# One expert's overflow rows take their second product in another place, and the tiles of finished rows get eight homes

## The reference

```
ys  = cond / sqrt(512);  d = rsqrt((ys*ys) @ (Wc*Wc) + 1e-8)
xf  = ((x * ys) @ Wc) * d                     # x: 2 x 2048 x 512, 4096 tokens
top = argmax(softmax(xf @ gate_w.T))          # one of two experts per token
for e in 0, 1:
    masked = where(top == e, xf, 0)           # other tokens' rows are zero
    routed += relu(masked @ w1[e] + b1[e]) @ w2[e] + b2[e]
shared = relu(xf @ sw1 + sb1) @ sw2 + sb2     # 512 -> 2048 -> 512
out = x + routed + shared
```

## Time and profile before

| | |
|---|---|
| median of 3 runs | 1408.11 us (1404.99 to 1409.16) |
| profiled execution, its own time | 1408.37 us |
| its span (first to last instruction) | 1406.6 us |
| PE busy | 1367.4 us, 97% of the span |
| DVE, ACT, POOL busy | 1004.5, 679.7, 364.2 us |
| mean granted PE clock | 0.990 |
| DMA in the span | 334.54 MB, 238 GB/s |
| chain that ended last | PE 86%, DMA 6%, DVE 4%, issue 2% |

### The profile page before, as it was taken

The page is one execution under the profiler, slowest core; times in us unless marked ns, Lnnn a source line. Parts: engine busy times, 40 slices in busy tenths (PEclk is TensorE's granted clock), DMA queues, the critical chain, the costliest instruction groups (busy, mean ns, idle before and its releaser), DMA issues.

```text
span 1406.6 us, 17366 instructions
## 1 busy us (share of the span) xinstructions
PE 1367.4 (97%) x5990; PEld 1126.0 (80%) x5990; DVE 1004.5 (71%) x1424; ACT 679.7 (48%) x988; POOL 364.2 (26%) x328
## 2 busy tenths in 40 slices
PE   9999999999989999899999999999999999897997
PEld 7888888888868788787888888888888887785886
DVE  7979967667788967966557878777897758453331
ACT  4456644545455544665666444444564445231220
POOL 0000005544636544250000000000000032354884
PEclk9999999999999999999999999999999999998999
DMA  6967475776877578653668887978787899997762
GB/s 206 285 244 223 181 250 189 252 231 251 268 257 260 209 255 272 229 181 129 213 224 281 262 281 251 290 254 272 258 250 244 273 291 320 290 298 178 215 163 33
DMA packets 243449, 334.54 MB, mean 238 GB/s; under 512 B 71760, under 2 KB 106576, under 8 KB 243088
## 3 DMA queue, kind: packets, MB, share of 16 engines
q1 hardware_dynamic: 216592, 299.58, 64.7%
q0 software_dynamic: 21248, 30.30, 9.8%
q10 hardware_dynamic: 5520, 3.54, 0.8%
HBM read 201.25 MB, written 149.29 MB: 249 GB/s over the span
## 4 chain that ended last, share of the span: by engine, by line
PE 86%; DMA 6%; DVE 4%; issue 2%; POOL 1%; ACT 1%; POOLq 0%; DVEq 0%; ACTq 0%; SPq 0%
PE bank L2015 39%; PE bank L2093 30%; PE bank L2122 8%; PE bank L1943 6%; DMA rows<-xf_scratch,quad_tab 1%; DMA y_rows<-x_rows,tab 1%; DMA hin<-hidden_scratch 1%; DMA out<-y_rows,tab 1%; DMA hin<-expert_hidden 1%; DVE vb L1512 1%; PE bank L2034 1%; DVE xw L1448 0%; DMA y_rows<-sorted_rows_out 0%; PE bank L2135 0%; DVE hl L1479 0%
## 5 line engine op out<-in xcount | busy, mean ns | idle before, releaser
L2015 PE MATMUL bank<-xw,w_hi 128*128 128x512 f32 x1792 | 555.9, 392 | 14.3 <-DVE vb L1512 12.2
L2093 PE MATMUL bank<-hl,w_hi 128*128 128x512 f32 x1344 | 414.4, 389 | 2.4 <-DVE hl L1479 2.2
L2015 PEld LDWEIGHTS bank<-xw,w_hi 128*128 128x128 f32 x1792 | 337.9, 189 | 86.8 <-DVE vb L1512 13.8
L1479 DVE TENSOR_TENSOR hl<-hin,hl 128x512 fp32r<-128x512 f32 x400 | 265.1, 686 | 197.5 <-ACT hl L1037 189.9
L1037 ACT CAST hl<-hin 128x512 fp32r<-128x512 f32 x400 | 244.6, 621 | 323.0 <-PE bank L2093 185.1
L2015 PE MATMUL bank<-xw,w_lo 128*128 128x512 f32 x896 | 350.4, 391 | 0.0
L2093 PEld LDWEIGHTS bank<-hl,w_hi 128*128 128x128 f32 x1344 | 251.8, 188 | 56.5 <-issue 3.5
L2093 PE MATMUL bank<-hl,w_lo 128*128 128x512 f32 x672 | 261.4, 389 | 0.0
L2015 PEld LDWEIGHTS bank<-xw,w_lo 128*128 128x128 f32 x896 | 169.3, 189 | 35.7
L1061 ACT ACTIVATE vb<-bank,b 128x512 f32<-128x512 f32 x192 | 130.2, 688 | 115.9 <-PE bank L2015 92.7
L882 POOL DMA_INDIRECT rows<-xf_scratch,quad_tab x128 | 129.6, 1012 | 150.4 <-PE bank L2015 105.2
(11 more groups left out here) (199 smaller groups left out, 1337.1 us busy)
## 6 DMA issues: line engine op xcount, KB each, us to landing
hin<-hidden_scratch SPq DMA_DIRECT2D x168, 512.0 KB
hidden_scratch<-vb SPq DMA_DIRECT2D x120, 512.0 KB
hidden_scratch<-vt SPq DMA_DIRECT2D x48, 512.0 KB
hin<-expert_hidden SPq DMA_DIRECT2D x32, 512.0 KB
w_new<-w_shared SPq DMA_DIRECT2D x52, 256.0 KB, 5.4
expert_hidden<-vb SPq DMA_DIRECT2D x24, 512.0 KB
ring<-x_cols SPq DMA_DIRECT2D x32, 256.0 KB
xf_scratch<-xo SPq DMA_DIRECT2D x32, 256.0 KB, 4.8
```

Of the source, the lines that this page charges most:

```text
L1479: nc.vector.tensor_tensor(hl[:, n % HL, 1, :], hin[:, n // 2 % LOADS, n % 2, :], hl[:, n % HL, 0, :].bitcast(F32), ALU.subtract).then_inc( ...
L2015: last = nc.tensor.matmul(up_bank(u, UP_BANK[c])[p][:], w[:, DOWN_W[c], pair, part], xw[:, c, x, k, :], start=(c in FRESH and n == 1), sto ...
L2093: last = nc.tensor.matmul(bank[p][:], w[:, DOWN_W[c], i, part], hl[:, n % HL, h, :], start=(i == 0 and q == 0), stop=(i == PAIRS - 1 and q ...
```

## The change

1. **Expert 0's overflow rows** go down from the weights of the seven products while those lie there: at the start of the last down block, (5, 0). `loose_set` on PE does 8 + 16 + 8 + 16 matmuls per unit and DVE four additions. It is within an `If` on `spilled[0]`. Loading and splitting `hv` moves for both experts: the load to (4, 6, 1), the split to (5, 0, 1) on ACT and (5, 0, 2) on DVE. PE then waits for both engines' mark before the block's first product.
2. **Expert 0's plain weights** go: four loads of 1 MB, 8 casts on ACT and 8 subtractions on DVE. Expert 1's overflow stays at (1, 8).
3. **Result tiles** have eight homes, in slot 7 of the two weight stores (56 to 62 KB and 120 to 126 KB), for all eight batches in turn. A batch's load waits for the additions of x of the batch before and for the writes of the batch before that; writes of odd batches have semaphores of their own (`odd_out`). `hv_halves` share no memory with them, and the wait for batch 3 goes.
4. **Places of the batches:** `TAIL_AT` and `TAIL_BATCHES` change.

```diff
-TAIL_BATCHES = ((2, 3), (4,), (5, 6), (7,))
-TAIL_AT = (5, 10, 19, 23, 27, 31)
+TAIL_BATCHES = ((2, 3), (4, 5), (6, 7), ())
+TAIL_AT = (7, 9, 17, 19, 23, 27)
-        y_rows = [at(kb, f"y_rows{i}", [D]) for i, kb in enumerate((200, 202, 208, 210))]
+        y_rows = [at(kb, f"y_rows{i}", [D]) for i, kb in enumerate((56, 58, 60, 62, 120, 122, 124, 126))]
@@ SP, tail_load
                 if batch == NT // 2 // RING:
-                    sp.wait_ge(loose_down_done, 2)
+                    sp.wait_ge(loose_down_done, 4)
                     sp.wait_ge(loose_filled, DMA * (2 + SPILL_TILES))
                 for i in range(RING):
                     k = RING * batch + i
-                    sp.wait_ge(sorted_out[i], DMA * (sorts_of[i] + batch))
+                    if batch > 0:
+                        sp.wait_ge(sorted_in[i], DMA * (sorts_of[i] + batch))
+                    if batch > 1:
+                        sp.wait_ge(*tail_left(batch - 2, i))
@@ ACT, down blocks
+                        if (s, c, i) == (FULL - 2, STEPS - 1, 1):
+                            act.wait_ge(loose_filled, 2 * DMA)
+                            loose_hidden_load(0)
+                        if (s, c, i) == (FULL - 1, 0, 1):
+                            loose_hidden_hi(0)
+                        if (s, c, i) == (FULL - 1, 0, LOOSE_SET):
+                            with act.If(spilled[0] > 0):
+                                with act.Fori(0, spilled[0]) as x:
+                                    loose_down(0, x)
+                            nc.scalar.copy(primed[:], ones[:, 0:1]).then_inc(loose_down_done, 1)
@@ ACT, wide stages
-                    if (wide, j) in WE_HI_LATE:
-                        we_cast(*WE_HI_LATE[wide, j])
-                    if (wide, j) == (LOOSE_DOWN[0], 12):
-                        for i in range(RING):
-                            act.wait_ge(sorted_out[i], DMA * (sorts_of[i] + NT // 2 // RING))
-                        loose_hidden_hi(0)
@@ PE
+            def loose_set(x):
+
+                bank, part = down_bank(FULL - 1, 0)
...
+                    if (s, c) == (FULL - 1, 0):
+                        with pe.If(spilled[0] > 0):
+                            with pe.Fori(0, spilled[0]) as x:
+                                loose_set(x)
+                        pe.wait_ge(loose_down_done, 2)
                     down_step(s, c)
@@ PE, at LOOSE_DOWN
-                        pe.wait_ge(we_lo, 4 * W)
-                        for e in range(2):
-                            with pe.If(spilled[e] > 0):
-                                with pe.Fori(0, spilled[e]) as x:
-                                    loose_down(e, x)
+                        with pe.If(spilled[1] > 0):
+                            with pe.Fori(0, spilled[1]) as x:
+                                loose_down(x)
```

More of the change, by code:

```diff
@@ L336, in build @@
         hin_in = [sem(f"hin_in{i}") for i in range(LOADS)]
[L337 removed]
+        we_in = w_raw_in
+        odd_out = [sem(f"odd_out{i}") for i in range(RING)]
         aux_in = sem("aux_in")
@@ L721, in tail_load @@
             def tail_load(batch):
+                if batch == 0:
+                    for i in range(2):
+                        sp.wait_ge(b11_out[i], DMA * GU // 2)
+                    sp.wait_ge(t1_out, DMA * GU)
+                    sp.wait_ge(b22_out, DMA * GU)
                 if batch == NT // 2 // RING:
-                    sp.wait_ge(loose_down_done, 2)
+                    sp.wait_ge(loose_down_done, 4)
                     sp.wait_ge(loose_filled, DMA * (2 + SPILL_TILES))
@@ L798, in _ @@
             for i in range(RING):
-                sp.wait_ge(sorted_out[i], DMA * (sorts_of[i] + COLS // RING - NT // 2 // RING))
+                for batch in (COLS // RING - NT // 2 // RING - 2, COLS // RING - NT // 2 // RING - 1):
+                    sp.wait_ge(*tail_left(batch, i))
         @block.gpsimd
@@ L1215, in keep_part, with loose_hidden_load, loose_hidden_hi, loose_down @@
                     nc.scalar.copy(v[:, 0, :, p, :], by_token(down_bank(s, 0)[p])).then_inc(dn_kept, 1)
+            def loose_hidden_load(x):
+                act.dma_start(hv[:], loose_unit(x)).then_inc(hv_in, DMA)
+            def loose_hidden_hi(x):
+                act.wait_ge(hv_in, DMA * (x + 1))
+                wait(act, loose_y_mm, (HC + 1) * x)
+                for half in range(2):
+                    part = slice(half * PAIRS, (half + 1) * PAIRS)
+                    nc.scalar.copy(hv_halves[half][:, :, 0, :], hv[:, part, :]).then_inc(hv_hi, 1)
+            def loose_down(e, x):
+                act.wait_ge(hv_lo, 2 * x + 2)
+                loose_hidden_load(x + 1)
+                act.wait_ge(loose_sum, 2 * x + 2 if e else 4 * x + 4)
+                act.wait_ge(loose_filled, DMA * (2 + CAP // P))
+                act.dma_start(loose_out[bass.ds(x * S, S), :], res_u[0:S, :]).then_inc(loose_stored, DMA)
+                act.wait_ge(loose_stored, DMA * (x + 1))
+                loose_hidden_hi(x + 1)
             for s in range(FULL):
@@ L1241, in last_part @@
                                   v[q * B32:(q + 1) * B32, c, :, :, :].rearrange("p j a b -> p j (a b)")).then_inc(v_out[c], DMA)
[L1243 to L1263, removed]
             for wide in range(WIDES):
@@ L2134, in loose_down @@
                     half = hv_halves[j // PAIRS]
-                    last = nc.tensor.matmul(bank[:], half[:, j % PAIRS, :, :], we_tile(w8_hi, e, j), start=(j == 0), stop=(j == HC - 1))
+                    last = nc.tensor.matmul(bank[:], half[:, j % PAIRS, :, :], we_tile(w8_hi, 1, j), start=(j == 0), stop=(j == HC - 1))
                 last.then_inc(loose_y_mm, 1)
@@ L2138, in loose_down @@
                     half = hv_halves[j // PAIRS]
-                    nc.tensor.matmul(bank[0:S, :], half[:, j % PAIRS, 0, :], we_tile(w8_lo, e, j), start=False, stop=(j == HC - 1),
+                    nc.tensor.matmul(bank[0:S, :], half[:, j % PAIRS, 0, :], we_tile(w8_lo, 1, j), start=False, stop=(j == HC - 1),
                                      skip_group_check=True).then_inc(loose_y_mm, 1)
```

132 lines of the change are left out of this document (75 added, 57 removed).

## The result

| | before | after |
|---|---|---|
| median of the runs | 1408.63 us (1404.99 to 1410.18) | 1392.68 us (1391.41 to 1395.06) |
| profiled execution, its span | 1408.37, 1406.6 us | 1393.44, 1391.7 us |
| PE busy | 1367.4 us, 97% | 1364.6 us, 98% |

The ratio is 0.990, 95% interval 0.9887 to 0.9914: faster by 16 us. Beside each other again, in the experiments, before took 1406.7 us and after 1392.2, which is 14.6. The forecast was 1396.5, in a range of 1392 to 1401: 11.7 us were expected to go, and 14.6 to 16 went.

A forecast was written before the change was run, and what follows sets the result against it. PE, busy 97% of the span, was taken as the bound. From 1408.37 us, 11.7 went for batch 3's wait (8.6) and half clock (3.0), all other terms 0: 1396.7, stated as 1396.5; range 1392 to 1401.

The forecast's parts named there:

- The branch: Overflow branches: this input has one unit of expert 1 and none of expert 0, so `loose_set` is never entered.
- The wait for batch 3 (8.6 us) and its half clock (3.0 us): Overflow unit at (1, 8): PE starts without the wait and at full clock, 11.7 us gained.
- The load and split of `hv` (0): Ahead of the last down block: load lands early, split ready 1.4 us before PE asks; 0, bound 2.9 us.
- The empty branches and the batches' places (0): A branch costs PE 0 to 0.7 us, one added, one gone; batches and hidden units keep room; 0.
- Expert 0's plain weights (0): Wide stages: removed loads, casts and subtractions give PE no time; 0, other bound 6.3 us.
- the waits near 1188 and 1204 us still there with their size: Sign in the profile after: PE's waits around the first wide stage unchanged, the second 4.63 us.
- a sign of being wrong: Prediction is wrong if PE's wait at 1204 us, ahead of the first wide stage, has gone or grown.
- My rival for this: Removed 1 MB load also relieves PE's wait at 1204: 1390.2 at most, 1393 for half; chance 0.07.

The follow-up runs named there:

- four_homes_again: split_waits with each batch's load also waiting for the writes of the batch before it, as with four homes; 1398.39 us.
- split_waits: Kernel after plus a second split of the overflow rows at the old place, behind batch 3's writes, with PE waiting for it; 1394.02 us.
- hv_late: Kernel after with the load of the overflow rows moved from (4, 6, 1) to right ahead of the split at (5, 0, 1); 1397.79 us.
- old_places: Kernel after with `TAIL_BATCHES` and `TAIL_AT` of the kernel before; 1391.72 us.
- after_again: Kernel after run once more, unchanged, beside other experiments; 1392.18 us.
- before_no_weights: Kernel before without expert 0's four plain-weight loads, 8 casts, 8 subtractions and its overflow branch at (1, 8); 1400.18 us, ratio 0.9951.
- swap_after: Kernel after with the two overflow counts exchanged, so the one unit is done as expert 0's; 1410.88 us.
- swap_before: Kernel before with the two overflow counts exchanged, so the one unit is done as expert 0's; 1413.97 us.
- moved_homes: before_no_weights with the four homes at 56 to 62 KB in place of 200, 202, 208 and 210; 1400.69 us.
- after_loads_first: Kernel after with, on SP's queue, the last down block's final hidden-unit loads ahead of batch 1's and its v stores behind two wide-stage loads; 1393.10 us.

## Why the prediction was right, and where it was off

*The branch.* Right: no product of `loose_set` ran in after.

*The wait for batch 3 (8.6 us) and its half clock (3.0 us).* Right in size: after's unit has no wait and runs at full clock, and the two kernels that keep a wait there show it beside ones that do not (four_homes_again is 4.4 us above split_waits, and PE loses 6.3 us at the unit in it, against 0.3). The mechanism was ACT's wait for the writes, as said.

*The load and split of `hv` (0).* Right. DVE's mark came at 1118.60 (forecast 1118.5), and hv_late shows what the eight casts ahead of it are worth: 5.6 us.

*The empty branches and the batches' places (0).* Right for the places (old_places is 0.5 us under after_again, which is within the noise). Batch 4's first add came at 1284.56 where I had 1290, and POOL's work ended 2 us before the forecast 1370. The branches show no wait.

*Expert 0's plain weights (0), and "the waits near 1188 and 1204 us still there with their size".* This is the step that was off, and in its second half. The prediction counted a wait at 1204 that has gone or grown as a sign of being wrong, and it fell from 4.63 to 1.16 us. The spans differ by 14.9 us. The unit is 11.6 of them; from 1160 to 1210 PE lost 10.1 us in before and 5.9 in after, so 4.2 more lie there; ahead of 1100 after lost 0.7 us more, and its end behind PE's last matmul is 0.2 longer. So PE ends 15.2 us earlier, where 11 to 12 were said. My rival for this named the removed load as the cause. Both experiments on it say no: put back, it costs 0.1 us of wait; taken out of before, it leaves the wait at 3.85. What the cause is stays open, and that the time still fell into the range is owed to the range's width, not to a term of the sum. The traces favour the homes' place: the lost time from 1160 to 1210 is 10.1 and 9.6 us in before and before_no_weights, with homes at 200 to 210 KB, and 5.7 to 7.3 in seven kernels with homes at 56 KB and up. Left out of that count are the three that move a load or a store in the last down block, and the two with exchanged counts. Of these swap_after speaks against it: its homes are at 56 KB and up, and from 1160 to 1250 it lost 12.2 us, where swap_before lost 9.3. The times do not favour it either: moved_homes is no faster than before_no_weights. With one profile each, a spread from run to run is not excluded (the wait went from 0.87 to 2.72 us in kernels that are the same up to there). The number of homes is not the cause by itself: four_homes_again lost 7.0 us there.

*What else the weights cost.* I took 0 for the three loads in the wide stages because PE had no wait beside them. before_no_weights shows 6.6 us, of which 6.2 at the unit: for part 2 alone my step would have been wrong. In the whole change it did no harm, since the wait that carried the price is gone.

## What to carry to other kernels

A transfer that delays nothing in its own stage can be paid for at a later wait that depends on the queue it lies in: follow the queue past it, not only the engine beside it. When a chain has a wait, several edits can each shorten or remove it, and their gains do not add; run each alone. Before moving an engine's loads ahead, look at what else that engine, and the one which consumes them, has to issue in the same stretch.

## What the runs showed of the hardware that I had not expected

- Half clock does not go with the length of a wait alone. Behind 3.10 us (four_homes_again, at 1187.76) and behind 2.24 and 2.72 us (old_places) PE's pace was full; behind 1.95 us (after_again) and 3.08 us (hv_late) it fell, which cost 1.6 and 2.9 us. The granted clock of a window that held little but such a stretch was 0.50, that is 1.2 GHz (after_loads_first, 1206 to 1212 us):

```profile
1206.00:1212.00 6.00, 5.41 (x13) 4.25 (x14) 5.97 (x9) 2.94 (x6) 2.45 (x2) 0.50 1.14 247
```

- Issuing four stores of 128 KB held ACT for 8.71 us in after_loads_first, with the DMA engines at share 1.08 (1196 to 1206 us). The fourth alone took 6.82 us, the others 0.34 to 0.75. In after the median of the eight such issues is 0.54 us and the longest, again the fourth, 3.02. Why the fourth is slow no run shows.
